# Attention of a two-layer block on one core: the rows of softmax shifts are turned by VectorE in 32x32 squares instead of by TensorE and ScalarE, both parts of the maxima are made by VectorE instead of GpSimd, and the PSUM bank of a score tile rotates by head without a wrap

## The chip, the core and the metric

The kernel runs on 1 core of a Trainium2 chip. The metric is device time in microseconds (us) of one execution. An engine is TensorE (PE; its weight loads are PEld), VectorE (DVE), ScalarE (ACT), GpSimd (POOL) or SyncE (SP, which issues most DMAs).

## The reference, cut to what matters

Two layers on 2048 tokens of width 128: a state-space layer with a routed feed-forward part, then attention with a second routed part. The change touches the attention alone:

```
q, k = rope(x @ Wq + bq), rope(x @ Wk + bk)     # 16 heads of width 8, 2048 tokens
p    = softmax(q @ k.T / sqrt(8))               # per head, 2048 x 2048
out  = concat(p @ v) @ Wo + bo
```

The kernel takes each query's largest score off before the exponential, as a softmax must where scores may be large.

## The kernel before, in words

**Three matmul streams a head.** `q_stack` and `k_stack` hold q and k of one head split in bfloat16 parts; the upper 64 partitions hold one half of the queries, the lower 64 the other, so that two matmuls with 64 rows of weights can run beside each other.
1. *Maxima* (`maxima`, L945): 64 score tiles of 128 queries x 512 keys per head (`SN = 64`), each in one PSUM bank. They serve to find each query's largest score. Head h+1's tiles are made while head h is worked on, 8 tiles in advance: two of them in each entry (below), the *upper* one ahead of the entry's score matmuls and the *lower* one behind them. After the first head they use a ring of three banks (4, 5, 6; `bank_of`), and `free` makes TensorE wait, before it writes a tile, until the tile three places back has been read.
2. *Scores* (`scores`, L956): for each of 16 key tiles (`kt`) and each half of the queries (`hf`), two matmuls give 128 keys x 1024 queries in two banks. One such (kt, hf) is an *entry*; a head has 32. The banks are used in two *slots* that alternate. ScalarE makes the exponentials of an entry in one instruction (L1339).
3. *Values* (`values`, L966): float32 matmuls of the exponentials with v, some entries later.

**Reading the maxima.** In program order of each eight tiles (p = 0 to 7 of a group): ScalarE reads p0 (a rectifier, `above`, L1331); VectorE reduces p1 to p5 and p7 to a column of maxima (L2044), and joins p6 with ScalarE's p0 in one instruction (L2040). VectorE so reads seven tiles of eight. After 32 tiles (`row_maxima`, called after p = 33) and after 64 it reduces the columns of half a head to one maximum for each query (`row_max`, 128 x 8, L2020).

**From maxima to shift rows.** The maxima stand one to a partition and are wanted as rows of `q_stack`, so that the score matmul subtracts them. GpSimd splits `row_max` in a high and a low bfloat16 part (`row_maxima` in its `attention`, L1535 and L1537, into `max_parts`). TensorE then turns 16 columns into 16 rows with a matmul against the identity (`row`, L951), which takes one of the two slots for a moment; ScalarE copies the 16 x 128 result to `shift_rows` (`row`, L1323); SyncE loads it into two places of `q_stack` (`load_rows`, L581; for the second half of head 0 ScalarE issues this load). This stands twice in a head, after `kt` 8 and after `kt` 14 (`ROWS_AFTER`), between two entries on TensorE and on ScalarE; the head then has 34 entries (`ENTRIES`), counted by `s2_ps` and `p_ready`. TensorE waits for the rows (`rows_in`) before entries 0 and 1 of the head that uses them.

**Order around it.** All engines run lists written out by hand, in order. SyncE's list for head h is: store head h-1, load both row halves of head h+1, wait for the last score of head h, load q and k of head h+4. Head 0's tiles are made ahead of the loop with six banks, with ScalarE and VectorE reading in turn; its first row stands after p = 44 (`FIRST_ROW`), its second after three tiles of head 1.

**The ring at a head's end.** The bank of tile p of head hs is

```
4 + (hs % UN + p) % RING        # UN = 4, RING = 3, 64 tiles a head
```

so tile 63 of heads 3, 7 and 11 and tile 0 of the next head have the same bank.

Of the kernel before, what the change touches and what calls it, by code (L numbers as in the profile page):

```python
# [31 lines left out]
TPC = C // 128  # L32
# [86 lines left out]
WIDES = [3, 9]  # L119
PADS = 6  # L120
# [47 lines left out]
ROWS_AFTER = (8, 14)  # L168
FIRST_ROW = SN // 2 + 12
ABOVE = 3  # L170
ROWS = 2 * SHIFT * TPC
ROW_LOADS = 16 * 2

# [5 lines left out]
def bank_of(hs, p):  # L179
    return 4 + (hs % UN + p) % RING if hs else FIRST_BANKS[p % len(FIRST_BANKS)]  # L180
# [32 lines left out]
ENTRIES = 2 * KT + 2  # L213


def entry(kt, hf, rows=True):
    return 2 * kt + hf + (rows and sum(kt > after for after in ROWS_AFTER))


ROW = [entry(after, 1) + 1 for after in ROWS_AFTER]  # L220


# [4 lines left out]
def build(nc, xT_in, cols_in, mats_in, wmod_in, bcsel_in, router_in, digits_in, cos_in, sin_in, spread_in, place_in, moe_in, out):  # L227
    with ExitStack() as ctx:
# [98 lines left out]
        max_parts = sb("max_parts", [128, 2, 2, SHIFT, TPC], BF16)  # L327
# [182 lines left out]
        row_max_ready, max_hi_ready, max_parts_ready = (sem(n) for n in ("row_max_ready", "max_hi_ready", "max_parts_ready"))  # L510
# [94 lines left out]
        def _(sp):  # L605
# [27 lines left out]
            def attention():  # L633
# [36 lines left out]
                load_rows(sp, 0, 0, 0, 3)  # L670
# [20 lines left out]
                for h in range(NH):  # L691
                    if h:
                        store_head(h - 1)
                    if h + 1 < NH:
                        for hf in range(2):
                            load_rows(sp, h + 1, (h + 1) % UN, hf, h * ENTRIES + (ROW[hf] + 5))
                    if h + UN < NH:
                        sp.wait_ge(s2_ps, h * ENTRIES + ENTRIES + 2)
                        load_q(sp, h + UN, h % UN)
                        load_k(sp, h + UN, h % UN)  # L700
# [39 lines left out]
        def _(pe):  # L740
# [171 lines left out]
            def attention():  # L912
# [46 lines left out]
                def values(h, u, kt, rows, part=None):  # L959
# [3 lines left out]
                    pe.wait_ge(p_ready, h * ENTRIES + (entry(kt, 1, rows) + 5))  # L963
# [7 lines left out]
                def late_values(h, u, kt, hf, rows):  # L971

                    at = 2 * kt + hf
                    if at == 0 and h:
                        values(h - 1, (u - 1) % UN, KT - 2, True, 1)
                    elif at == 1 and h:
                        values(h - 1, (u - 1) % UN, KT - 1, True)
                    elif at == 3:
                        values(h, u, 0, rows)
                    elif at > 4:  # L980
                        values(h, u, kt - 2 + hf, rows, 1 - hf)

                def head(h, u, turn, following=NH):
# [7 lines left out]
                    for kt in range(KT):  # L991
                        for hf in range(2):
# [3 lines left out]
                            n = entry(kt, hf, following)  # L996
                            if kt == 0:
                                pe.wait_ge(rows_in[hf], h * ROW_LOADS + ROW_LOADS)
                            pe.wait_ge(p_ready, h * ENTRIES + (n + 3))
# [3 lines left out]
                            late_values(h, u, kt, hf, following)  # L1003
                        if following and kt in ROWS_AFTER:
                            hf = ROWS_AFTER.index(kt)
                            row(h + 1, hf, h * ENTRIES + (2 + ROW[hf]), ROW[hf] % 2)
                for p in range(SN):
                    if p == FIRST_BANKS.index(1):
                        pe.wait_ge(v_all_ready, TILES)
                    if p == FIRST_ROW:  # L1010
                        row(0, 0, 0, 0)
                    maxima(0, 0, p)
                for p in range(RING):
                    maxima(1, 1, p)
                row(0, 1, 1, 1)
                for p in range(RING, 2 * LEAD):
# [3 lines left out]
                values(NH - 1, UN - 1, KT - 2, False, 1)  # L1020
                values(NH - 1, UN - 1, KT - 1, False)

            def attention_out():
                busy(psum[:, 4, :], 26)
                pe.wait_ge(inv_ready, 1)
                pe.wait_ge(p_ready, 2 + 2 + ENTRIES * NH - 2)
# [140 lines left out]
        def _(act):  # L1167
# [139 lines left out]
            def attention():  # L1307
# [25 lines left out]
                def exponentials(h, kt, hf, rows=True):  # L1333
                    n = entry(kt, hf, rows)
                    slot = n % 2
                    act.wait_ge(s2_ps, h * ENTRIES + (n + 3))
# [10 lines left out]
                for p in range(SN):  # L1347
                    if p == FIRST_ROW:
                        row(0, 0, 0, 0)
# [3 lines left out]
                row(0, 1, 1, 1)  # L1353
                load_rows(act, 0, 0, 1, 4)
                for h in range(NH):
                    following = h + 1 < NH
                    for kt in range(KT):
# [3 lines left out]
                        for hf in range(2):  # L1361
                            exponentials(h, kt, hf, following)
                        if kt == 0 and h:
                            keep(h - 1)
                        if following and kt in ROWS_AFTER:
                            hf = ROWS_AFTER.index(kt)
                            row(h + 1, hf, h * ENTRIES + (2 + ROW[hf]), ROW[hf] % 2)
# [75 lines left out]
        def _(pool):  # L1443
# [43 lines left out]
            def attention_inputs():  # L1487
                pool.wait_ge(ln_in_ready, 3 * NC)
                g.memset(no_shift[:], 0.0).then_inc(pool_made, 1)
                g.memset(v_head[:], 0.0).then_inc(pool_made, 1)  # L1490
# [29 lines left out]
            def attention():  # L1520
# [6 lines left out]
                def row_maxima(hs, hf):  # L1527
                    n = hs * 2 + (hf + 1)
                    tiles = slice(8 * hf, 8 * hf + 8)
                    pool.wait_ge(row_max_ready, n)  # L1530
                    if hs:

                        pool.wait_ge(s2_ps, hs * ENTRIES + (2 - ENTRIES))
                    whole, (high, low) = row_max[:, tiles, 0].rearrange("p (d j) -> p d j", j=TPC), (max_parts[:, hf, :, n, :] for n in range(SHIFT))
                    g.tensor_tensor(high, whole, no_shift[:], ALU.add).then_inc(max_hi_ready, 1)  # L1535
                    pool.wait_ge(max_hi_ready, n)
                    g.tensor_tensor(low, whole, high, ALU.subtract).then_inc(max_parts_ready, 1)  # L1537

                def head(h, u, more=True):
                    for hf in range(2):  # L1540
                        row_maxima(h, hf)
# [58 lines left out]
        def _(dve):  # L1600
# [410 lines left out]
            def attention():  # L2011
# [3 lines left out]
                def row_maxima(hs, hf):  # L2015
                    tiles = slice(8 * hf, 8 * hf + 8)
                    dve.wait_ge(s1_read, reads(hs, SN // 2 * (hf + 1)))
                    dve.wait_ge(max_parts_ready, hs * 2 + (hf + 1))
                    tops = tile_max if hs else first_max
                    v.tensor_reduce(row_max[:, tiles, 0], tops[:, tiles, :], AX.X, ALU.max).then_inc(row_max_ready, 1)  # L2020

# [7 lines left out]
                def head(hs):  # L2029
                    for p in range(SN):  # L2030
# [22 lines left out]
                for h in range(NH):  # L2053
                    head(h)
                dve.wait_ge(o_in, 32)
# [101 lines left out]
```

## Time and profile before

| what | us |
|---|---|
| time, median of 3 runs (lowest to highest) | 1195.78 (1195.12 to 1197.62) |
| span of the profiled execution, first to last instruction | 1191.5 |
| attention's steady part, 16 heads, in the profiled execution | about 429 to 1025 |
| busy in the span: TensorE, VectorE, ScalarE, GpSimd | 1039.4, 853.0, 798.2, 291.2 |

No separate time is given for the profiled execution; its span is 4.3 us below the median of the runs. A busy share is a mean over stages with different limits, so the attention has to be read by itself; engines that are busy the same share of a stretch can still be bounded by only one of them.

### The profile page before, as it was taken

What the parts mean: (1) busy time and instruction counts of PE and PEld (TensorE: products, weight loads), DVE (VectorE), ACT (ScalarE), POOL (GpSimd) and SP (SyncE); (2) the same over time, 40 slices, a digit from 0 to 9 for tenths busy, and PEclk for the clock granted to TensorE, in tenths of its full rate; (3) what the DMA queues carried; (4) which work ended last, traced back from release to release, by engine and by line L of the source; (5) the groups of instructions that cost most, each with busy time, mean ns of one, the idle gap of its engine ahead of it and who ended that gap; (6) DMA issues with size and microseconds to landing.
All of it is one profiled execution on the core that took longest, in us unless ns stands there. A gap on an engine that the chain in (4) does not pass through costs nothing.

```text
span 1191.5 us, 22203 instructions
## 1 busy us (share of the span) xinstructions
PE 1039.4 (87%) x8296; PEld 485.1 (41%) x8300; DVE 853.0 (72%) x1585; ACT 798.2 (67%) x1206; POOL 291.2 (24%) x296
## 2 busy tenths in 40 slices
PE   9936767787989689999999999999999999968795
PEld 6512224786964222222222222222222222448694
DVE  2499997347135689999999999999999992362222
ACT  2653333455545469999999999999999999431122
POOL 0069881655334500000000000000000000026652
PEclk7969998889888879999999999999999999988997
DMA  3056530866642310011100111001110100038683
GB/s 104 1 166 195 179 122 36 260 189 201 186 136 88 122 61 25 12 34 34 34 16 20 34 34 34 9 27 34 34 34 2 33 4 4 4 126 266 204 268 124
DMA packets 49110, 104.16 MB, mean 87 GB/s; under 512 B 9440, under 2 KB 11864, under 8 KB 48620
## 3 DMA queue, kind: packets, MB, share of 16 engines
q1 hardware_dynamic: 43386, 91.76, 24.6%
q0 software_dynamic: 4544, 9.32, 2.4%
q10 hardware_dynamic: 1074, 1.67, 0.4%
q8 instruction: 66, 1.08, 0.4%
q14 instruction: 40, 0.33, 0.1%
HBM read 89.35 MB, written 12.94 MB: 86 GB/s over the span
## 4 chain that ended last, share of the span: by engine, by line
PE 61%; issue 12%; DVE 9%; ACT 9%; DMA 4%; POOL 2%; another core or an unknown queue 1%; SPq 1%; ACTq 0%; DVEq 0%; POOLq 0%
PE psum L966 19%; PE psum L945 12%; PE psum L956 8%; PE psum L1085 6%; PE psum L1096 6%; ACT probs L1339 5%; DVE tile_max L2044 2%; DVE ssm_h L1764 1%; PE psum L789 1%; PE psum L1068 1%; PE psum L769 1%; DMA y_in<-y_dram 1%; ACT ln_xn L1331 1%; POOL h0T L1483 1%
## 5 line engine op out<-in xcount | busy, mean ns | idle before, releaser
L1339 ACT ACTIVATE probs<-psum 128x1024 f32<-128x1024 f32 x512 | 504.2, 1041 | 27.6 <-PE psum L956 22.3
L2044 DVE TENSOR_REDUCE tile_max<-psum 128x1 f32<-128x512 f32 x720 | 459.8, 685 | 31.8 <-PE psum L945 25.1
L945 PE MATMUL psum<-k_stack,q_stack 62*128 62x512 bf16 x994 | 313.3, 388 | 14.1 <-DMA q_stack<-q_dram 8.6
L966 PE MATMUL psum<-probs,v_head 128*32 128x256 f32 (+1 forms) x3840 | 321.0, 406 | 0.6 <-ACT probs L1339 0.4
L956 PE MATMUL psum<-q_stack,k_stack 64*128 64x512 bf16 x1024 | 290.0, 384 | 10.6 <-ACT probs L1339 8.7
L945 PEld LDWEIGHTS psum<-k_stack,q_stack 62*128 62x128 bf16 x994 | 77.4, 94 | 242.7 <-issue 109.7
L966 PEld LDWEIGHTS psum<-probs,v_head 128*32 128x32 f32 x3840 | 75.7, 108 | 164.6 <-issue 126.0
L1535 POOL TENSOR_TENSOR max_parts<-row_max,no_shift 128x8 bf16<-128x8 f32 x32 | 6.4, 200 | 557.0 <-DVE row_max L2020 557.0
L1096 PE MATMUL psum<-w2r,hid 128*128 128x128 f32 x624 | 92.5, 296 | 25.4 <-issue 25.2
L1085 PE MATMUL psum<-x_cols,w1r 128*128 128x128 f32 (+1 forms) x624 | 93.5, 299 | 8.8 <-issue 8.0
L1096 PEld LDWEIGHTS psum<-w2r,hid 128*128 128x128 f32 x624 | 84.3, 210 | 28.0 <-issue 27.6
L1085 PEld LDWEIGHTS psum<-x_cols,w1r 128*128 128x128 f32 x624 | 86.0, 213 | 10.7 <-issue 9.8
L1418 ACT ACTIVATE hid<-psum 128x512 f32<-128x512 f32 x39 | 23.0, 597 | 94.3 <-PE psum L1085 49.0
L1483 POOL TENSOR_TENSOR h0T<-dtuT,ssm_b 128x1024 f32<-128x1024 f32 x32 | 76.9, 2414 | 16.4 <-DVE ssm_h L1764 7.3
L1570 POOL DMA_INDIRECT y_dram<-o_rows,put_row x64 | 62.9, 983 | 68.4 <-ACT o_rows L1388 36.4
L1562 POOL DMA_INDIRECT x_got<-xtok_dram,get_row x64 | 63.0, 984 | 52.9 <-issue 34.3
L850 PE MATMUL psum<-ssm_g,mats 128*128 128x512 f32 x128 | 62.7, 614 | 11.5 <-POOL ssm_g L1457 6.4
L2040 DVE CUSTOM_DVE_ANT_0 proj_o<-psum,ln_xn 128x512 f32<-128x512 f32 x100 | 67.8, 684 | 6.5 <-PE psum L945 6.3
L1331 ACT ACTIVATE ln_xn<-psum 128x512 f32<-128x512 f32 x100 | 58.9, 593 | 18.7 <-PE psum L941 11.8
L956 PEld LDWEIGHTS psum<-q_stack,k_stack 64*128 64x128 bf16 x1024 | 55.2, 94 | 36.8 <-ACT probs L1339 31.3
L1900 DVE COPY o_rows<-psum 128x128 f32<-128x128 f32 x39 | 11.3, 290 | 80.7 <-PE psum L1096 44.1
L1246 ACT ACTIVATE psum<-dtT,negA 128x1024 f32<-128x1024 f32 x32 | 35.4, 1109 | 28.6 <-DVE ssm_h L1764 19.0
(287 smaller groups left out, 1107.5 us busy)
## 6 DMA issues: line engine op xcount, KB each, us to landing
w1r<-w SPq DMA_DIRECT2D x78, 256.0 KB
w2r<-w SPq DMA_DIRECT2D x78, 256.0 KB
ssm_b<-bc_dram SPq DMA_DIRECT2D x32, 512.0 KB, 4.0
k_stack<-k_dram SPq DMA_DIRECT2D x60, 120.0 KB
y_in<-y_dram SPq DMA_DIRECT2D x16, 256.0 KB, 5.1
q_stack<-q_dram SPq DMA_DIRECT2D x30, 96.0 KB
bc_p<-bc_dram SPq DMA_DIRECT2D x5, 512.0 KB, 5.7
xtok_dram<-x_tok SPq DMA_DIRECT2D x8, 256.0 KB, 2.4
```

The lines of the kernel that those rows point to most:

```text
L945: mm(bank, queries, k_stack[rows, u, keys:keys + C], start=True, stop=True).then_inc(s1_ps, 1)
L956: return mm(psum[:, 2 * slot + side, :], k_stack[rows, u, kt * 128:(kt + 1) * 128], q_stack[rows, u, hf * C:(hf + 1) * C], start=True, sto ...
L966: i = mm(psum[32 * j:32 * j + VM, 7, lo:hi], v_head[:, u, kt, :], probs[:, kt % 4, j * C + lo:j * C + hi], start=kt == 0, stop=kt == KT - ...
L1085: j = mm(psum[:, n % 3, hc * 128:(hc + 1) * 128], w1r[:, k, hc * 128:(hc + 1) * 128], space, start=True, stop=True)
L1096: j = mm(psum[:, 6 + n % 2, 0:128], hid[:, n % 2, hc, :], w2r[:, k, hc, :], start=hc == 0, stop=hc == HC - 1)
L1331: f(above_next[n % ABOVE], psum[:, bank_of(hs, p), :], ACT.Relu).then_inc(above_ready, 1)
L1339: f(probs[:, kt % 4, hf * HALF:(hf + 1) * HALF], banks(2 * slot, 2), ACT.Exp, scale=SCALE).then_inc(p_ready, 1)
L1483: g.tensor_tensor(ssm_dBu[:, n % 2, :], half(dtuT, hf), ssm_b[:, n % B_RING, :], ALU.mult).then_inc(dBu_ready, 1)
L1562: g.indirect_dma_start(x_got[:, k, :], None, xtok_dram, bass.IndirectOffsetOnAxis(get_row[:, i:i + 1], 0)).then_inc(got[k], 16)
L1570: g.indirect_dma_start(y_dram, bass.IndirectOffsetOnAxis(rows, 0), o_rows[:, k, :], None).then_inc(put[k], 16)
L2040: v.tensor_tensor_reduce(proj_o[:, r % 2, :], bank, above_next[r % ABOVE], 1.0, LOWEST, ALU.add, ALU.max, top).then_inc(s1_read, 1)
L2044: v.tensor_reduce(top, bank, AX.X, ALU.max).then_inc(s1_read, 1)
```

## The change

The matmul, the copy and the entry for a row go. VectorE makes the high and the low part (two `tensor_tensor` of 128 x 8) into a zeroed 128 x 32 tile `max_squares`, and turns this tile with four 32 x 32 transposes, one for each 32 partitions, into 32 partitions of `shift_rows`, of which 16 are used. These instructions stand in VectorE's list of tile reads: for the first half behind p = 34 (high), 35 (low) and 36 (four transposes); for the second half behind p = 0, 1 and 2 of the next head. After head 15's last tile the second half's follow directly. The loads wait for `max_turned`. A head has 32 entries again. The bank uses `hs` instead of `hs % UN`. GpSimd clears `max_squares` once and no longer takes part.

```diff
-ROWS_AFTER = (8, 14)
-FIRST_ROW = SN // 2 + 12
+TURN_AFTER = (SN // 2 + 4, 2)
+SQUARE = 32
+SQUARES = 128 // SQUARE
 def bank_of(hs, p):
-    return 4 + (hs % UN + p) % RING if hs else FIRST_BANKS[p % len(FIRST_BANKS)]
+    return 4 + (hs + p) % RING if hs else FIRST_BANKS[p % len(FIRST_BANKS)]
-ENTRIES = 2 * KT + 2
+ENTRIES = 2 * KT
-        max_parts = sb("max_parts", [128, 2, 2, SHIFT, TPC], BF16)
+        max_squares = sb("max_squares", [128, 2, SQUARE], BF16)
+        max_parts = max_squares[:, :, 0:ROWS].rearrange("p h (d s j) -> p h d s j", d=2, s=SHIFT)
...
-        def load_rows(eng, h, u, hf, done):
-            eng.wait_ge(p_ready, done)
+        def load_rows(eng, h, u, hf):
+            eng.wait_ge(max_turned, SQUARES * (2 * h + hf + 1))
...
-                def row(hs, hf, g, slot):
-                    pe.wait_ge(max_parts_ready, hs * 2 + (hf + 3))
-                    pe.wait_ge(p_ready, g + 1)
-                    mm(psum[0:ROWS, 2 * slot, 0:128], max_parts[:, hf].rearrange("p d s j -> p (d s j)"), ident_b[:],
-                       start=True, stop=True).then_inc(s2_ps, 1)
...
-                def row(hs, hf, g, slot):
-                    act.wait_ge(s2_ps, g + 1)
-                    if hs:
-                        act.wait_ge(rows_in[hf], hs * ROW_LOADS)
-                    f(shift_rows[0:ROWS, hf, :], psum[0:ROWS, 2 * slot, 0:128], ACT.Identity).then_inc(p_ready, 1)
...
-                def row_maxima(hs, hf):
-                    pool.wait_ge(row_max_ready, n)
...
-                    g.tensor_tensor(high, whole, no_shift[:], ALU.add).then_inc(max_hi_ready, 1)
-                    pool.wait_ge(max_hi_ready, n)
-                    g.tensor_tensor(low, whole, high, ALU.subtract).then_inc(max_parts_ready, 1)
...
+                def part_maxima(hs, hf, low):
...
+                    if low:
+                        dve.wait_ge(max_parts_ready, 2 * n + 1)
+                        v.tensor_tensor(rest, whole, high, ALU.subtract).then_inc(max_parts_ready, 1)
+                        return
+                    dve.wait_ge(row_max_ready, n)
+                    if hs:
+                        dve.wait_ge(max_turned, SQUARES * (n - 2))
+                    v.tensor_tensor(high, whole, no_shift[:], ALU.add).then_inc(max_parts_ready, 1)
+                def turn_maxima(hs, hf):
+                    dve.wait_ge(max_parts_ready, hs * 4 + (hf * 2 + 4))
+                    if hs:
+                        dve.wait_ge(rows_in[hf], hs * ROW_LOADS)
+                    for g in range(SQUARES):
+                        at = slice(SQUARE * g, SQUARE * (g + 1))
+                        v.transpose(shift_rows[0:SQUARE, hf, at], max_squares[at, hf, :]).then_inc(max_turned, 1)
...
                         if p == SN // 2 + 1:
                             row_maxima(hs, 0)
+                        for k in range(2):
+                            if p == SN // 2 + 2 + k:
+                                part_maxima(hs, 0, k)
+                            if p == k and hs:
+                                part_maxima(hs - 1, 1, k)
+                        if p == TURN_AFTER[0]:
+                            turn_maxima(hs, 0)
+                        if p == TURN_AFTER[1] and hs:
+                            turn_maxima(hs - 1, 1)
```

## Rows read from the trace of the kernel before

Time and busy columns are in us from the span's start, means in ns. In a timeline an answer's line is: start, length, engine, line, operation, tiles and sizes, count, and in brackets the idle time before it and what ended it.

**Rows 1.** The page's first part: busy time, share of the span, instructions.
```profile
PE 1039.4 (87%) x8296; PEld 485.1 (41%) x8300; DVE 853.0 (72%) x1585; ACT 798.2 (67%) x1206; POOL 291.2 (24%) x296
```

**Rows 2.** Busy time of one head: us, busy PE, PEld, DVE, ACT, POOL, clock, DMA.
```profile
565.30:602.70 37.40, 36.73 (x375) 10.21 (x370) 35.20 (x67) 35.37 (x44) 1.06 (x5) 1.00 0.09 28
```

**Rows 3.** The page's second costliest group: busy, mean of one, idle before it.
```profile
L2044 DVE TENSOR_REDUCE tile_max<-psum 128x1 f32<-128x512 f32 x720 | 459.8, 685 | 31.8 <-PE psum L945 25.1
```

**Rows 4.** TensorE's timeline, two entries without a row: upper tiles, values.
```profile
571.49 0.39 PE L945 MATMUL psum<-k_stack,q_stack 62*128 62x512 bf16 x1
...
572.60 0.39 PE L945 MATMUL psum<-k_stack,q_stack 62*128 62x512 bf16 x1
...
573.16 0.64 PE L966 MATMUL psum<-probs,v_head 128*32 128x256 f32 x8
573.73 0.39 PE L945 MATMUL psum<-k_stack,q_stack 62*128 62x512 bf16 x1
```

**Rows 5.** TensorE's timeline around the second row (L951) of a head.
```profile
577.05 0.39 PE L945 MATMUL psum<-k_stack,q_stack 62*128 62x512 bf16 x1
...
578.19 0.39 PE L945 MATMUL psum<-k_stack,q_stack 62*128 62x512 bf16 x1
...
579.18 0.22 PE L951 MATMUL psum<-ident_b,max_parts 128*16 128x128 bf16 x1
579.33 0.39 PE L945 MATMUL psum<-k_stack,q_stack 62*128 62x512 bf16 x1
579.99 0.39 PE L956 MATMUL psum<-q_stack,k_stack 64*128 64x512 bf16 x2 [0.27 <-ACT probs L1339]
...
581.09 0.39 PE L945 MATMUL psum<-k_stack,q_stack 62*128 62x512 bf16 x1
```

**Rows 6.** ScalarE's timeline at the same row.
```profile
579.79 0.25 ACT L1323 ACTIVATE shift_rows<-psum 16x128 bf16<-16x128 f32 x1
580.42 1.02 ACT L1339 ACTIVATE probs<-psum 128x1024 f32<-128x1024 f32 x1 [0.38 <-PE psum L956]
```

**Rows 7.** VectorE's timeline: a group's only gap, then a head's second row maximum.
```profile
574.15 0.69 DVE L2044 TENSOR_REDUCE tile_max<-psum 128x1 f32<-128x512 f32 x1 [0.17 <-PE psum L945]
...
576.55 0.68 DVE L2040 CUSTOM_DVE_ANT_0 proj_o<-psum,rope_sin 128x512 f32<-128x512 f32 x1
...
577.16 0.69 DVE L2044 TENSOR_REDUCE tile_max<-psum 128x1 f32<-128x512 f32 x1
577.88 0.19 DVE L2020 TENSOR_REDUCE row_max<-tile_max 128x8 f32<-128x32 f32 x1
577.98 0.68 DVE L2044 TENSOR_REDUCE tile_max<-psum 128x1 f32<-128x512 f32 x1
```

**Rows 8.** TensorE's timeline at the end of head 3's tiles (same bank twice).
```profile
538.16 0.64 PE L966 MATMUL psum<-probs,v_head 128*32 128x256 f32 x8
539.67 0.37 PE L945 MATMUL psum<-k_stack,q_stack 62*128 62x512 bf16 x1 [0.87 <-DVE tile_max L2044]
```

**Rows 9.** The chain of waits, first and last of three like pieces.
```profile
535.83 1.43 DVE tile_max L2044 x3
...
837.01 1.43 DVE tile_max L2044 x3
```

**Rows 10.** VectorE's timeline far ahead of the attention: small operations, each waiting for the last.
```profile
241.97 0.16 DVE L1944 TENSOR_TENSOR thr_low<-thr_low,thr_add 128x1 int32<-128x1 int32 x1
242.17 0.16 DVE L1935 TENSOR_TENSOR thr_try<-thr_low,digits 128x1 int32<-128x1 int32 x1
```

**Rows 11.** The chain of waits at the start of the head loop.
```profile
424.87 0.20 DVE row_max L2020
...
426.23 0.75 ACTq L581
```

**Rows 12.** SyncE's timeline: the last load of head 1's k, then head 0's first rows.
```profile
414.09 0.29 SPq L575 DMA_DIRECT2D k_stack<-k_dram  x1
417.18 1.39 SPq L581 DMA_DIRECT2D q_stack<-shift_rows  x2
```

More of the change, by code:

```diff
@@ L210, with entry @@
 JOINED_READ = [reads(hs, p + 1) for hs in range(NH) for p in range(SN) if order_of(hs)[p][3] == JOINED]
-ENTRIES = 2 * KT + 2
-def entry(kt, hf, rows=True):
-    return 2 * kt + hf + (rows and sum(kt > after for after in ROWS_AFTER))
-ROW = [entry(after, 1) + 1 for after in ROWS_AFTER]
+ENTRIES = 2 * KT
+def entry(kt, hf):
+    return 2 * kt + hf
 def half_tiles(hf):
@@ L957, in scores, with values @@
                               q_stack[rows, u, hf * C:(hf + 1) * C], start=True, stop=True)
-                def values(h, u, kt, rows, part=None):
+                def values(h, u, kt, part=None):
                     if kt == 0:
@@ L962, in values @@
                         pe.wait_ge(o_copied, h + 1)
-                    pe.wait_ge(p_ready, h * ENTRIES + (entry(kt, 1, rows) + 5))
+                    pe.wait_ge(p_ready, h * ENTRIES + (entry(kt, 1) + 3))
                     lo, hi = (0, C) if part is None else (part * C // 2, (part + 1) * C // 2)
@@ L1002, in head @@
                             lower()
[L1003 to L1006, printed above, removed]
+                            late_values(h, u, kt, hf)
                 for p in range(SN):
@@ L1009, in attention @@
                         pe.wait_ge(v_all_ready, TILES)
-                    if p == FIRST_ROW:
-                        row(0, 0, 0, 0)
                     maxima(0, 0, p)
[L1013 to L1016, printed above, removed]
+                for p in range(2 * LEAD):
                     maxima(1, 1, p)
@@ L1019, in attention @@
                     head(h, h % UN, h // UN, following=NH - 1 - h)
-                values(NH - 1, UN - 1, KT - 2, False, 1)
-                values(NH - 1, UN - 1, KT - 1, False)
+                values(NH - 1, UN - 1, KT - 2, 1)
+                values(NH - 1, UN - 1, KT - 1)
             def attention_out():
@@ L1331, in above, with exponentials @@
                     f(above_next[n % ABOVE], psum[:, bank_of(hs, p), :], ACT.Relu).then_inc(above_ready, 1)
-                def exponentials(h, kt, hf, rows=True):
-                    n = entry(kt, hf, rows)
+                def exponentials(h, kt, hf):
+                    n = entry(kt, hf)
                     slot = n % 2
-                    act.wait_ge(s2_ps, h * ENTRIES + (n + 3))
+                    act.wait_ge(s2_ps, h * ENTRIES + (n + 1))
                     if hf == 0:
@@ L1352, in attention @@
                 above(1, 0)
[L1353 to L1354 removed]
+                load_rows(act, 0, 0, 1)
                 for h in range(NH):
[L1356 removed]
                     for kt in range(KT):
@@ L1361, in attention @@
                         for hf in range(2):
-                            exponentials(h, kt, hf, following)
+                            exponentials(h, kt, hf)
                         if kt == 0 and h:
                             keep(h - 1)
-                        if following and kt in ROWS_AFTER:
-                            hf = ROWS_AFTER.index(kt)
-                            row(h + 1, hf, h * ENTRIES + (2 + ROW[hf]), ROW[hf] % 2)
                 keep(NH - 1)
@@ L2017, in row_maxima @@
                     dve.wait_ge(s1_read, reads(hs, SN // 2 * (hf + 1)))
-                    dve.wait_ge(max_parts_ready, hs * 2 + (hf + 1))
+                    dve.wait_ge(max_parts_ready, max(hs * 4 + hf * 2, 2))
                     tops = tile_max if hs else first_max
                     v.tensor_reduce(row_max[:, tiles, 0], tops[:, tiles, :], AX.X, ALU.max).then_inc(row_max_ready, 1)
+                def part_maxima(hs, hf, low):
+                    n = hs * 2 + (hf + 1)
+                    tiles = slice(8 * hf, 8 * hf + 8)
+                    whole, (high, rest) = row_max[:, tiles, 0].rearrange("p (d j) -> p d j", j=TPC), (max_parts[:, hf, :, k, :] for k in range(SHIFT))
+                    if low:
[13 more added lines that the diff above has]
+                        v.transpose(shift_rows[0:SQUARE, hf, at], max_squares[at, hf, :]).then_inc(max_turned, 1)
                 bv = mat("bv_rows").rearrange("p (h d) -> p h d", h=NH)
@@ L2054, in attention @@
                     head(h)
+                for k in range(2):
+                    part_maxima(NH - 1, 1, k)
+                turn_maxima(NH - 1, 1)
                 dve.wait_ge(o_in, 32)
```

39 lines of the change are left out of this document (16 added, 23 removed).

## The prediction

> **What bounds the kernel now.** I read the busy totals first: TensorE is busy 87% of the span, VectorE 72%, ScalarE 67% [rows 1]. Then one head by stretch: in 37.4 us TensorE is busy 36.7, ScalarE 35.4 and VectorE 35.2, at a granted clock of 1.00, that is 2.4 GHz [rows 2]. Three engines lie within 2 us of each other, so shares can't tell which is the bound; the timelines must.
>
> TensorE's entries without a row start 1.11 us apart and follow each other without a pause: the values of one take 0.57 us until the next upper tile, the rest is scores and maxima [rows 4]. VectorE reads a tile every 0.60 to 0.61 us, one read takes 0.69 to its end, and in a group of eight tiles it has one gap, 0.17 us [rows 3, 7]. So TensorE sets the pace of an undisturbed group and VectorE is a little faster than it needs to be.
>
> The rows disturb it. With a row, TensorE's scores come 0.66 us behind their upper tile instead of beside it, and two entries take 2.90 us (578.19 to 581.09) instead of 2.22: a row costs 0.68 us [rows 5]. The matmul is only 0.22; the rest is the wait for ScalarE, which has to copy the row (0.25) and then waits itself for the scores (0.38) [rows 5, 6]. Two rows a head make 1.36 us of 37.4.
>
> One more stall stands at a head's end: behind the values the next upper tile comes after 1.51 us instead of 0.57, and 0.87 of it is idle, waiting for VectorE's read [rows 4, 8]. Here tile 63 and the next head's tile 0 have the same bank. The chain of waits shows the stall three times [rows 9].
>
> What is to be seen in that stall is the tightness of the ring: a tile's matmul can start only when the tile three back has been read, and a late read goes into TensorE's time at once, since nothing else can be taken out of its list.
>
> **The change, part by part.**
>
> *Rows off TensorE and ScalarE.* 15 heads follow with two rows each inside the loop: 30 x 0.68 = -20.4 us.
>
> *Bank by head.* Three stalls of about 0.9 go: -2.7 us. Late next would be the tile three back, read long before.
>
> *GpSimd's two operations* run beside everything; nothing is won, since only the row waited for them, and clearing the squares once stands in GpSimd's list ahead of its wait for the tables; without that cover it is one small operation, some 0.2 us.
>
> *VectorE's new work.* First what a small operation costs there. Unhindered, the next read starts 0.10 us behind `row_max`, though that is 0.19 long [rows 7]; I take 0.10 for each part. Where an operation waits for the one ahead, the full length and about 0.04 are paid: small ones of 0.16 follow in 0.20 [rows 10], and `row_max` itself starts 0.72 behind a read instead of 0.61 [rows 7].
>
> The transpose is in no row. Its lower bound is the 0.10 of an unhindered small operation, four of them 0.40. Its upper bound is full length, 0.19 + 0.03 = 0.22 [rows 7]: three such steps and 0.10 for the last, 0.76. Which is nearer? Every pair of VectorE operations that overlaps in this kernel's rows begins at partition 0 on all 128; the four transposes begin at partitions 0, 32, 64 and 96, so the overlap isn't shown for them. I take full length, T = 0.76, and keep 0.40.
>
> The Trainium skill, "VectorE: DVE Perf Modes", section "Two Vector instructions with no wait between them", has a rule on this: an instruction whose input or output starts in another group of 32 partitions than the last one's starts only when all earlier Vector instructions have finished. That speaks against this change; no run here shows it. By the rule T is 0.76, by the row of `row_max` alone 0.40; with the first the sum below is +8, with the second about -4.
>
> *First half of a head.* Take the group whose upper p0 starts at 0. VectorE reads p2 at 1.55 (574.15 less 572.60 [rows 4, 7]); high delays p3 by 0.10, low p4 by another 0.10, the transposes p5 by T. So p6 ends 0.20 + T later than it did. The next group's lower tile p1 needs p6's bank, and before it got it with nothing to spare: p6 is read from 576.55 for 0.68, and the next group's first entry already takes 1.14 instead of 1.11 [rows 4, 5, 7]. The delay goes into TensorE whole: +0.20 + T = 0.96.
>
> *Second half.* High stands directly behind `row_max`, with no read between, and waits for it: p1 moves from 577.98 to about 578.20. Then p1 0.60, low 0.10: p2 at 578.90. Before, p2 could start when its tile was there, 578.19 + 0.39 [rows 5] + about 0.03 = 578.61. That is +0.29, and T on top: +1.05. The gap that would have taken 0.17 was already used by `row_max`.
>
> Each head: 0.96 + 1.05 - 1.36 = +0.65; VectorE's work of 2.0 us exceeds what TensorE is freed of. For 15 heads +9.8 us.
>
> *Loads.* The last transpose of the second half ends at about 578.90 + 0.60 + 0.66 + 0.22 = 580.38; ScalarE's copy ended at 580.04 [rows 6]. SyncE's load so starts 0.34 later, and it is the next thing in that queue either way; TensorE wants the rows 0.37 later too (1.05 less 0.68), so the margin stays. VectorE's added waits, on the loads of a head ago, are over when it comes to them. Behind them its own tile reads are queued, and TensorE waits for those.
>
> *The start.* Head 0's second row now needs high, p1, low, p2 and the transposes behind `row_max`: about 0.22 + 0.10 + 0.60 + 0.10 + 0.60 + 0.88 = 2.5 us, where the load was issued 1.36 us behind it (424.87 to 426.23 [rows 11]): +1.1. Head 0's first half puts up to 0.96 into VectorE's reads. Against that SyncE, which stood idle from 414.38 to 417.18 for head 0's first row [rows 12], gets it earlier, and heads 2 and 3's loads move up by at most 2.8. Bounds -2.8 to +2.1; I take +1.
>
> **Sum:** +9.8 - 2.7 + 1 = +8 us. The profiled execution has a span of 1191.5 and no time of its own; 4.3 us lie between it and the median of the runs, and I take these as unchanged. So, 1195.8 + 8 = **1204 us**.
>
> **The rivals.**
>
> *A, cheap transposes.* They overlap like `row_max` and the read behind it. T = 0.40 gives 0.60 + 0.69 = 1.29 a head against 1.36: -1 in 15 heads, and with the banks, and nothing for the start, about -4: **1192**. This is the rival on the other side. Its place is the four transposes behind p = 36 and behind p = 2, its price 2T a head, and it decides from 15 x (0.49 + 2T - 1.36) - 1.7 = 0, that is T = 0.49. For it: every overlap in the rows. Against: those all stay on the same partitions.
>
> *B, the lag is absorbed.* VectorE has eight gaps of 0.17 a head, 1.36 us [rows 7]. If its lag is worked off in them without holding TensorE, only 2.0 - 1.4 = 0.65 of its new work shows: a head falls by 0.7, 15 heads by 10.7, and with -1.7 the time is **1183**. For it: the totals of the engines, VectorE's head comes to 37.2 us at most by busy time [rows 2]. Against: rows 8, where one late read idles TensorE for 0.87 with the gaps as they are.
>
> *C, the joined read waits too.* If an operation that changes partitions is paid at full length, the read of p6 behind the transposes, which takes ScalarE's tile from partition 0 on, may start 0.1 late as well (the 0.11 of `row_max` [rows 7]): 30 times, +3, **1207**. It is part of the likeliest case's own spread.
>
> **How the numbers follow.** Full length with or without C has 0.60; its own range is 1199 to 1211, from 0.2 a head on the delays and the bounds of the start. A has 0.27 (1189 to 1196), B 0.09; 0.04 is for what I don't see, split. The range that leaves 2 in 10 out goes from A's lower part to the top of the likeliest case: 1190 to 1211. A measurement of this kernel can tell about 0.2%, 2.4 us, from no change. Faster: B and 0.6 of A, 0.25. Within 0.2%: 0.35 of A and the lowest end of the likeliest case, 0.12. Slower: 0.63.
>
> **What the profile of after would show.** TensorE's L951, ScalarE's L1323 and GpSimd's two groups are gone, and no entry's scores start behind their upper tile for want of a slot. Heads no longer differ by 0.9 after heads 3, 7 and 11. VectorE's four transposes in a row start about 0.22 apart (right) or 0.10 (rival A). Behind each set, TensorE's maxima wait for VectorE's reads, about 1 us per half head, and a head takes 38.0 us. If a head takes 37.3 with transposes 0.10 apart, A holds; if transposes are slow and a head still takes under 37, the step that puts VectorE's delay whole into TensorE is wrong. I am wrong altogether if the transposes cost several times their length, or if the rows reach `q_stack` too late and TensorE waits for the load.

## The result and the profile after

The changed kernel is slower: 1201.26 us median (1198.07 to 1211.46, 13 runs) against 1191.30 (1185.09 to 1197.62, 13 runs) of the kernel before on the same chip, a ratio of 1.0090 with a 95% interval of 1.0068 to 1.0112. That is +8 to +13 us, where +8 was forecast.

The two profiled executions lie further apart than the medians, 1209.6 against 1191.5 of span, and part of that is not the change's: the profiled execution of after is the slowest of its 13 runs (1211.46), and GpSimd's first `q_negative`, which closes the work ahead of the attention, ends at 406.26 against 401.43. All comparisons below start there. From that point to the reciprocal of the softmax sums at the attention's end, the kernel before takes 629.45 and the one after 642.25: **+12.8 us**. With the 4.8 ahead of it and 0.5 behind it, that is the 18.1 between the spans. One execution of each is not a mean: a run below whose edit leaves the start alone shows a start 1.7 longer than before's, so +12.8 and the +10 of the medians don't disagree.

The page of after, its first part and two groups (busy, mean ns of one, idle before it and what ended most of it):

```profile
PE 1046.0 (86%) x8264; PEld 484.2 (40%) x8268; DVE 876.8 (72%) x1777; ACT 802.6 (66%) x1174; POOL 279.9 (23%) x233
...
L2024 DVE TENSOR_REDUCE tile_max<-psum 128x1 f32<-128x512 f32 x720 | 458.0, 681 | 25.9 <-PE psum L946 24.7
...
L946 PEld LDWEIGHTS psum<-k_stack,q_stack 62*128 62x128 bf16 x994 | 79.9, 93 | 291.5 <-DVE tile_max L2024 182.5
```

The last group in the page of before:

```profile
L945 PEld LDWEIGHTS psum<-k_stack,q_stack 62*128 62x128 bf16 x994 | 77.4, 94 | 242.7 <-issue 109.7
```

The tile reads cost what they cost before (681 ns against 685 [rows 3]), but 192 instructions have joined them on VectorE (1777 against 1585 [rows 1]): 16 heads x 2 halves x 6. The weight loads name the victim: TensorE's for the maxima now sat idle mostly for VectorE's reads (182.5 of 291.5), where before the largest part (109.7 of 242.7) had no wait that the profile shows ("issue").

One head, from its first exponential to that of the next (busy by engine as in [rows 2]):

```profile
593.60:631.90 38.30, 37.20 (x372) 10.21 (x374) 36.57 (x79) 35.73 (x42) 0.32 (x1) 1.00 0.09 27
```

38.30 against 37.42, at the same clock. VectorE is busy 1.37 longer than before (36.57 against 35.20), TensorE 0.47 (37.20 against 36.73), and TensorE now stands idle for 1.10 of the head where it was 0.67. The waits of two heads, before (565 to 640) and after (594 to 668), each with its sum in us, its count and the longest:

```profile
PEld psum L945 <- DVE tile_max L2044: 12.3, 27, 0.8
```

```profile
PEld psum L946 <- DVE tile_max L2024: 23.0, 50, 0.9
```

The weight loads wait twice as often for VectorE. Where that comes from is seen in VectorE's timeline after a first half's maximum:

```profile
608.88 0.16 DVE L1992 TENSOR_TENSOR max_squares<-row_max,no_shift 128x8 bf16<-128x8 f32 x1
608.96 0.68 DVE L2024 TENSOR_REDUCE tile_max<-psum 128x1 f32<-128x512 f32 x1
609.56 0.16 DVE L1987 TENSOR_TENSOR max_squares<-row_max,max_squares 128x8 bf16<-128x8 f32 x1
609.63 0.68 DVE L2024 TENSOR_REDUCE tile_max<-psum 128x1 f32<-128x512 f32 x1
610.23 0.88 DVE L2000 STREAM_TRANSPOSE shift_rows<-max_squares 32x32 bf16<-32x32 bf16 x4
611.05 0.64 DVE L2024 TENSOR_REDUCE tile_max<-psum 128x1 f32<-128x512 f32 x1
611.72 0.69 DVE L2020 CUSTOM_DVE_ANT_0 proj_o<-psum,ln_xn 128x512 f32<-128x512 f32 x1
```

The parts cost 0.08 and 0.07 each: the read behind one starts so soon although the part is 0.16 long. The four transposes hold the engine from 610.23 to the next read at 611.05, **0.82**. And the joined read (L2020) starts 0.67 behind its predecessor, 0.03 after that one's end, where reads of before follow in 0.60 to 0.61 [rows 3, 7]. In heads 1 to 13 all 26 joined reads behind transposes start 0.03 after their predecessor's end, and all 78 others 0.08 before it. TensorE pays at the upper tiles:

```profile
610.07 0.39 PE L946 MATMUL psum<-k_stack,q_stack 62*128 62x512 bf16 x1
...
611.75 0.39 PE L946 MATMUL psum<-k_stack,q_stack 62*128 62x512 bf16 x1 [0.41 <-ACT probs L1318]
...
613.37 0.39 PE L946 MATMUL psum<-k_stack,q_stack 62*128 62x512 bf16 x1
```

Two entries take 1.68 and 1.62 instead of 1.11 [rows 4]: +1.08. (The bracket names ScalarE, but the upper tile at 611.75 is p = 40 and needs the bank of p = 37, whose read ended at 611.05 + 0.64 = 611.69. The lower tile behind it, at 612.48, needs that of p = 38, the joined read, which ended at 611.72 + 0.69 = 612.41.) In the second half three entries from 627.86 on take 1.67, 1.49 and 1.33: +1.16. Together 2.24, less the 1.36 of the two rows: +0.88 a head, and heads 1 to 13 all take 38.29 to 38.30. The 38.32 that heads 2, 6 and 10 took before (at their ends the tiles of heads 3, 7 and 11 give way to the next head's) is gone with the repeated bank.

At the start, the chain of waits shows the transposes one by one, then the load of head 0's second row (start, us, what):

```profile
430.20 0.20 DVE row_max L1979
430.40 0.02 issue
430.42 0.17 DVE max_squares L1992
430.59 0.60 DVE tile_max L2024
431.19 0.07 DVE max_squares L1987
431.26 0.60 DVE tile_max L2024
431.86 0.11 DVE shift_rows L2000
431.97 0.03 issue
432.00 0.20 DVE shift_rows L2000
432.20 0.03 issue
432.23 0.18 DVE shift_rows L2000
432.41 0.06 issue
432.46 0.21 DVE shift_rows L2000
432.67 0.02 issue
432.70 0.75 ACTq L582
433.44 0.04 issue
433.48 6.14 DMA q_stack<-shift_rows
```

Each transpose runs to its end before the next starts: they start 0.23 apart (432.00, 432.23, 432.46). The load is issued 2.50 behind `row_max`, against 1.36 before [rows 11].

Where the +12.8 came from, added up along ScalarE's first exponentials and TensorE's wait for that load: 2.92 up to head 0's second entry, 1.04 from there to head 1, 13 x 0.87 = 11.3 in heads 1 to 13, -2.7 by the banks, and 0.24 in heads 14 and 15. Head 14 by itself doesn't change (36.03 against 36.04).

### The profile page after: what moved, and what is told of

Its sections match the earlier page's. It is cut to its first block, busy times and chain, and to the rows that moved or that the text cites. A ratio compares the mean times of both kernels' runs of the same rounds, so it can differ in the third digit from the quotient of the medians.

```text
span 1209.6 us, 22204 instructions
## 1 busy us (share of the span) xinstructions
PE 1046.0 (86%) x8264; PEld 484.2 (40%) x8268; DVE 876.8 (72%) x1777; ACT 802.6 (66%) x1174; POOL 279.9 (23%) x233
## 3 DMA queue, kind: packets, MB, share of 16 engines
q10 hardware_dynamic: 1074, 1.67, 0.4%
q8 instruction: 66, 1.08, 0.4%
## 4 chain that ended last, share of the span: by engine, by line
PE 59%; DVE 13%; issue 13%; ACT 6%; DMA 4%; POOL 2%; SPq 1%; another core or an unknown queue 0%; ACTq 0%; DVEq 0%; POOLq 0%
PE psum L960 18%; PE psum L946 12%; PE psum L950 7%; PE psum L1071 6%; PE psum L1082 6%; ACT probs L1318 4%; DVE tile_max L2024 2%; DVE proj_o L2020 2%; DVE ssm_h L1723 2%; PE psum L790 1%; PE psum L1054 1%; DVE shift_rows L2000 1%; DMA y_in<-y_dram 1%; PE psum L770 1%; POOL h0T L1455 1%
## 5 line engine op out<-in xcount | busy, mean ns | idle before, releaser
L946 PE MATMUL psum<-k_stack,q_stack 62*128 62x512 bf16 x994 | 320.6, 390 | 26.6 <-ACT probs L1318 12.2
L950 PE MATMUL psum<-q_stack,k_stack 64*128 64x512 bf16 x1024 | 296.8, 385 | 3.8 <-DMA q_stack<-shift_rows 3.4
L946 PEld LDWEIGHTS psum<-k_stack,q_stack 62*128 62x128 bf16 x994 | 79.9, 93 | 291.5 <-DVE tile_max L2024 182.5
L1498 POOL COPY v_head<-v_all 128x144 f32<-128x144 f32 x16 | 5.0, 318 | 476.6 <-PE psum L960 476.6
L1310 ACT ACTIVATE ln_xn<-psum 128x512 f32<-128x512 f32 x100 | 59.0, 594 | 25.3 <-PE psum L946 11.3
L1859 DVE COPY o_rows<-psum 128x128 f32<-128x128 f32 x39 | 11.3, 289 | 81.5 <-PE psum L1082 39.8
L2020 DVE CUSTOM_DVE_ANT_0 proj_o<-psum,ln_xn 128x512 f32<-128x512 f32 x100 | 67.8, 683 | 0.8 <-ACT ln_xn L1310 0.2
L1377 ACT ACTIVATE hid<-psum,block_b 128x128 f32<-128x128 f32 x128 | 36.8, 383 | 26.6 <-PE psum L1071 19.9
```

The costliest lines, as they stand in the source:

```text
L946: mm(bank, queries, k_stack[rows, u, keys:keys + C], start=True, stop=True).then_inc(s1_ps, 1)
L950: return mm(psum[:, 2 * slot + side, :], k_stack[rows, u, kt * 128:(kt + 1) * 128], q_stack[rows, u, hf * C:(hf + 1) * C], start=True, sto ...
L2020: v.tensor_tensor_reduce(proj_o[:, r % 2, :], bank, above_next[r % ABOVE], 1.0, LOWEST, ALU.add, ALU.max, top).then_inc(s1_read, 1)
```

## The experiments

The theory after the result: the four transposes are paid at full length because each reads other partitions than the one before, and whatever VectorE loses there TensorE loses too. Rivals: the parts are what costs (not the transposes); the transposes are that slow anyway; the ring's lead is too short; the start carries the loss (of this the sum above leaves at most 2.92 of 12.8). Each run's times were compared with the kernel before on the same chip; heads are measured between first exponentials.

**The banks alone**, in the kernel before.

```diff
-    return 4 + (hs % UN + p) % RING if hs else FIRST_BANKS[p % len(FIRST_BANKS)]
+    return 4 + (hs + p) % RING if hs else FIRST_BANKS[p % len(FIRST_BANKS)]
```

> The kernel before with the new bank rule alone. Theory: the three stalls at the ends of heads 3, 7 and 11 (0.90 us each, a head of 38.32 against 37.42) go and nothing else moves: all heads 37.42 us, -2.7 us, 0.23% faster than before. Rival: with the wrap gone the lag of VectorE's reads shows elsewhere in those heads and less than 1 us is won.

Measured: 1184.25 against 1186.64, ratio 0.9987 (0.9969 to 1.0005). ScalarE's timeline at the starts of heads 2, 3 and 4 (head 2 is the first that took 38.32 before):

```profile
499.93 1.03 ACT L1339 ACTIVATE probs<-psum 128x1024 f32<-128x1024 f32 x1
...
537.36 1.03 ACT L1339 ACTIVATE probs<-psum 128x1024 f32<-128x1024 f32 x1
...
574.78 1.03 ACT L1339 ACTIVATE probs<-psum 128x1024 f32<-128x1024 f32 x1
```

37.43 and 37.42, and so are all heads from 1 to 13: the three stalls go, -2.7 us in the trace, and no head is longer in their place. The time can't tell -2.7 from nothing, since its interval holds both 0.9977 and 1. In this execution the way to head 1 was 1.7 longer than before's (70.25 against 68.54), which no part of the edit touches, so stretches at the start differ by that much between executions.

**Four transposes that all read partitions 0 to 31.**

```diff
-SCALE = float(HD) ** -0.5
+SCALE = 0.05
...
-    v.transpose(shift_rows[0:SQUARE, hf, at], max_squares[at, hf, :]).then_inc(max_turned, 1)
+    v.transpose(shift_rows[0:SQUARE, hf, at], max_squares[0:SQUARE, hf, :]).then_inc(max_turned, 1)
```

> The changed kernel, but all four transposes read partitions 0 to 31 (so three quarters of the shifts are other queries' maxima, and the exponential's scale is made 0.05 to keep its results finite). Theory: a transpose starts late because it begins at other partitions than the one ahead of it; here the four start 0.10 us apart and the joined read behind them starts 0.60 instead of 0.67 to 0.70 behind its predecessor; a half head gains 3 x 0.12 + 0.1, a head falls from 38.29 to about 37.35 us. Rival: transposes never overlap; they start 0.22 apart as in the changed kernel and a head stays at 38.1 to 38.3.

The shifts of three quarters of the queries are other queries' here, so only the times count. It ran once, 1189.35 against 1186.64, from which nothing follows; in the profiled execution the attention, measured as above, takes 623.54 against before's 629.45. VectorE's timeline in the same place as above:

```profile
563.11 0.68 DVE L2024 TENSOR_REDUCE tile_max<-psum 128x1 f32<-128x512 f32 x1
563.71 0.47 DVE L2000 STREAM_TRANSPOSE shift_rows<-max_squares 32x32 bf16<-32x32 bf16 x4
564.11 0.64 DVE L2024 TENSOR_REDUCE tile_max<-psum 128x1 f32<-128x512 f32 x1
564.68 0.67 DVE L2020 CUSTOM_DVE_ANT_0 proj_o<-psum,rope_sin 128x512 f32<-128x512 f32 x1
```

The same four instructions now take 0.40 (563.71 to 564.11) instead of 0.82, each 0.09 to 0.12 behind the last, and the joined read starts 0.57 behind its predecessor instead of 0.67. Heads take 37.21 instead of 38.29: 1.08 less, of which 2 x 0.42 are the transposes and 2 x 0.10 the joined reads. The only other edit is the scale inside ScalarE's exponentials, so the change of partitions is the price, of both. This is also rival A's case made on the chip: at T = 0.40 a head is 0.21 shorter than the 37.42 of before.

The Trainium skill, "VectorE: DVE Perf Modes", section "Two Vector instructions with no wait between them", says that an instruction is held until all earlier ones have finished when an input starts in another group of 32 partitions than the last input read from the same memory. The traces agree in each part: the second to fourth transposes are held, the first isn't; the read behind them (its input in PSUM) isn't; the joined read, the next to read SBUF, is, and it reads from partition 0 where the last transpose read from 96. The prediction told the rule as a comparison with the last instruction, whatever that one read; by those words the read of PSUM behind the transposes would be held too, and it starts 0.06 before the last transpose ends.

**The parts back on GpSimd**, transposes kept.

```diff
+    g.tensor_tensor(high, whole, no_shift[:], ALU.add).then_inc(max_parts_ready, 1)
+    pool.wait_ge(max_parts_ready, 2 * n + 1)
+    g.tensor_tensor(low, whole, high, ALU.subtract).then_inc(max_parts_ready, 1)
...
-    for k in range(2):
-        if p == SN // 2 + 2 + k:
-            part_maxima(hs, 0, k)
-        if p == k and hs:
-            part_maxima(hs - 1, 1, k)
```

> The changed kernel with the high and the low part made by GpSimd again; VectorE keeps the transposes. Theory: what VectorE no longer does comes off TensorE's stalls whole: 0.20 us in the first half, 0.22 + 0.10 in the second; a head falls from 38.29 to about 37.8, the kernel by 7 to 8 us against the changed one, to about no difference from before. Rival: VectorE then waits for GpSimd ahead of the transposes and a head stays at 38.3 or grows.

Measured: 1193.49 against 1186.64, ratio 1.0072 (1.0045 to 1.0099); heads 37.89. The parts so cost 0.40 of a head on VectorE, and without them the change is still slower than before. The rival that the parts are the whole loss falls. The head is as expected, the time is not: about no difference from before was expected, and heads of 37.89 against 37.42 alone make 13 x 0.47 - 2.7 = +3.4. The start makes the rest. It was longer than in any run but one (head 1 at 72.89): GpSimd's first high part, behind its own 5.46 us addition to `xT`, came at 409.30 where `row_max` was at 404.97, and VectorE's transposes waited for it (68.54 to head 1 in before).

**The first half's work spread to VectorE's gaps**: high behind p = 41, low behind 49, transposes behind 57, where a group's first read has 0.17 to spare [rows 7].

```diff
-TURN_AFTER = (SN // 2 + 4, 2)
+TURN_AFTER = (SN // 2 + 25, 2)
...
-    if p == SN // 2 + 2 + k:
+    if p == SN // 2 + 9 + 8 * k:
         part_maxima(hs, 0, k)
```

> The changed kernel with the first half's work at other places: high behind p = 41, low behind p = 49, the four transposes behind p = 57, each where VectorE has its 0.17 us gap in a group. Theory: only the lag that the gap doesn't take reaches TensorE: high and low cost nothing, the transposes 0.17 less; the first half's stall falls from 1.08 to about 0.7, a head from 38.29 to about 37.9, the kernel by 5 to 6 us against the changed one. Rival: what counts is VectorE's work in sum, wherever it stands; a head stays at 38.3.

Measured: 1189.75 against 1186.64, ratio 1.0038 (1.0022 to 1.0053); heads 37.87, that is 0.42 less than after. VectorE's timeline around the part and the transposes:

```profile
600.00 1.28 DVE L2024 TENSOR_REDUCE tile_max<-psum 128x1 f32<-128x512 f32 x2
601.20 0.16 DVE L1987 TENSOR_TENSOR max_squares<-row_max,max_squares 128x8 bf16<-128x8 f32 x1
601.45 2.48 DVE L2024 TENSOR_REDUCE tile_max<-psum 128x1 f32<-128x512 f32 x4
...
605.66 0.88 DVE L2000 STREAM_TRANSPOSE shift_rows<-max_squares 32x32 bf16<-32x32 bf16 x4
606.48 2.43 DVE L2024 TENSOR_REDUCE tile_max<-psum 128x1 f32<-128x512 f32 x4
608.94 0.69 DVE L2020 CUSTOM_DVE_ANT_0 proj_o<-psum,ln_xn 128x512 f32<-128x512 f32 x1
```

Behind the part the next read starts at 601.45, 0.17 after the end of the reads ahead (600.00 + 1.28), which is the gap of a group without it [rows 7]: there the part costs nothing. The transposes take 0.82 here too, and a gap of 0.17 takes back little of that. The joined read is late again: it starts 0.03 behind the end of the four reads between (606.48 + 2.43), where in the undisturbed group it starts 0.08 ahead of that end.

**GpSimd's addition to `xT` later.** In the trace of after, one instruction is out of line: the first high part of head 0. GpSimd's and VectorE's timelines there:

```profile
415.96 5.45 POOL L1509 TENSOR_SCALAR xT<-xT,gated_bo 128x2048 f32<-128x2048 f32 x1
...
417.75 1.96 DVE L1992 TENSOR_TENSOR max_squares<-row_max,no_shift 128x8 bf16<-128x8 f32 x1
419.62 0.68 DVE L2020 CUSTOM_DVE_ANT_0 proj_o<-psum,ln_xn 128x512 f32<-128x512 f32 x1
420.23 0.08 DVE L2020 DVE_READ_ACCUMULATOR2_ANT first_max<- 128x1 f32 x1
420.23 0.15 DVE L1987 TENSOR_TENSOR max_squares<-row_max,max_squares 128x8 bf16<-128x8 f32 x1
```

1.96 instead of 0.16, while GpSimd adds. The edit moves the addition into the loop over heads, at h = 2:

```diff
-    g.tensor_scalar(xT[:], xT[:], gated_bo[:], None, ALU.add).then_inc(x_biased, 1)
...
+    if h == 2:
+        g.tensor_scalar(xT[:], xT[:], gated_bo[:], None, ALU.add).then_inc(x_biased, 1)
```

> The changed kernel with GpSimd's 5.45 us addition to xT moved behind its copies of v for heads 2 to 4. Theory: head 0's first high part took 1.96 us instead of 0.16 because GpSimd's long operation ran beside it and VectorE's two-input operation had to wait for it; with that moved it takes 0.16 to 0.2, and the way from the end of GpSimd's q_negative to the first exponential is about 1.8 us shorter (29.4 to about 27.6 us, give or take the landing of loads); heads stay at 38.29. The moved addition may now hold one such operation of VectorE in the loop for up to 2 us. Rival: the first operation of its kind is slow whatever runs beside it; it stays at 1.96.

```profile
410.91 0.16 DVE L1993 TENSOR_TENSOR max_squares<-row_max,no_shift 128x8 bf16<-128x8 f32 x1
```

The part takes 0.16, the first exponential comes after 27.56 instead of 29.36, head 1 after 69.91 instead of 72.50, and heads stay at 38.29. So the two did collide, for 1.8. The time doesn't show it: 1201.69 against 1189.62, ratio 1.0101 (1.0061 to 1.0141), an interval that holds after's whole.

**One transpose of all 128 partitions** from head 1 on, 128 x 32 into 128 x 32, with eight small loads a half in place of two; the parts and the transposes at places with a gap; and, since the rows come later, a lead of eight entries.

```diff
-LEAD = 4
-TURN_AFTER = (SN // 2 + 4, 2)
+LEAD = 8
+TURN_AFTER = (SN // 2 + 25, 5)
...
+    for g in range(SQUARES):
+        first = SQUARE * g + side * SHIFT * TPC
+        part = to.rearrange("s (j g c) -> s j g c", g=SQUARES, c=SQUARE)[:, :, g, :]
+        eng.dma_start(part, shift_rows[first:first + SHIFT * TPC, hf, 0:SQUARE]).then_inc(rows_in[hf], 16)
...
+    v.transpose(shift_rows[:, hf, 0:SQUARE], max_squares[:, hf, :]).then_inc(max_turned, 1)
...
-    if p == SN // 2 + 2 + k:
+    if p == SN // 2 + 9 + 8 * k:
...
-    if p == k and hs:
+    if p == k + 1 and hs:
```

> The changed kernel with, from head 1 on, one transpose of 128 x 32 in place of four of 32 x 32 (the rows then stand in four places of 32 partitions and are loaded by eight DMAs for each half instead of two), the tiles made 16 instead of 8 in advance so that the loads have time, the first half's work in the gaps (high behind 41, low 49, transpose 57), the second's behind p = 1, 2 and 5. Theory: a transpose that stays on its partitions costs VectorE 0.1, and work in a gap costs nothing; a head keeps 37.42 - 1.36 and some 0.3 of the second half: 36.3 to 36.6 us, -13 to -16 us in 15 heads, -2.7 for the banks, +2 to +4 for eight more tiles ahead of the loop: 1.0 to 1.4% faster than before. Rival: the 16 DMA issues a head (0.65 us each on SyncE) land too late for entry 1 or collide with the stores, and heads stay above 37.4.

Measured: **1178.07 against 1189.62, ratio 0.9914 (0.9883 to 0.9946)**: faster than both kernels. VectorE's timeline at a first-half and a second-half transpose, then the head that begins at 570.26:

```profile
564.28 0.20 DVE L2015 STREAM_TRANSPOSE shift_rows<-max_squares 128x32 bf16<-128x32 bf16 x1
564.40 0.65 DVE L2039 CUSTOM_DVE_ANT_0 proj_o<-psum,ln_xn 128x512 f32<-128x512 f32 x1
...
593.61 0.20 DVE L2015 STREAM_TRANSPOSE shift_rows<-max_squares 128x32 bf16<-128x32 bf16 x1
```

```profile
570.26:606.82 36.56, 36.43 (x376) 10.28 (x368) 35.12 (x73) 35.42 (x42) 0.32 (x1) 1.00 0.10 28
```

One transpose of 128 partitions is as long as one of 32 (0.20), in the first half the next instruction, the joined read, starts 0.12 behind it and is on time. A head takes 36.56: 1.73 less than after, 0.86 less than before, and 1.0 above the 35.5 of 32 undisturbed entries. VectorE is busy 35.12 instead of 36.57. The 240 small loads stall TensorE little (0.5 us in two heads). How much of the 1.73 is the one transpose and how much the places isn't measured apart; the spread of the first half with four transposes gave 0.42.

The time fell by less than the 1.0 to 1.4% expected. In the profiled execution the attention takes 613.38 against 629.45, 16.1 less, but that execution is the fastest of the six (1170.60; the others 1176.39 to 1181.83); what the others lost has no trace.

**The lead alone**, in the kernel after (`LEAD = 8` and ScalarE's first reads to match), as the control.

```diff
-LEAD = 4
+LEAD = 8
...
-    above(1, 0)
+    for p in range(0, 2 * LEAD, GROUP):
+        above(1, p)
```

> The changed kernel with the tiles made 16 instead of 8 in advance and nothing else. Theory: where tiles stand in a head's entries doesn't matter to the ring, a head stays at 38.3; the first exponential comes later by about eight tiles, at most 5 us, part of which is given back at head 0's entry 1, that waits less for its rows, and at the end. Rival: the loads of the second half's rows were close to late; with more time for them heads shrink by some tenths.

Its one time is 1201.35: heads 38.29 to 38.30 as in after, and the attention 642.32 against 642.25. A longer lead brings the first exponential 4.64 later (34.00 against 29.36 behind `q_negative`), shortens head 0 by 3.38 (39.76 against 43.14) and head 14 by 1.04 (34.99 against 36.03), and changes nothing between. So the lead by itself gains nothing, and what the run with one transpose gained is put down to the transposes and the places; whether it would have held with a lead of four was not run.

## Why the prediction was right

- **Rows off TensorE and ScalarE, -0.68 each: consistent.** The row's entry was not measured alone, but with the delays read off TensorE's timeline it closes the head: 2.24 - 1.36 = 0.88 against 0.87 measured.
- **Banks, -2.7: right.** Shown in both kernels that have the edit.
- **Transposes at full length: right**, and the choice that decided the sign. T was 0.82 where 0.76 was taken, since the steps are 0.22 to 0.23 and the last one costs more than an unhindered small operation. At equal partitions T was 0.40, the other end to the hundredth, and a head then came to 37.21 where the prediction's working gives 37.35.
- **The parts: nearly right.** 0.10 was taken, 0.07 to 0.08 shown; taking them off saves 0.40 of a head against 0.49 in the sum.
- **VectorE's delay goes whole into TensorE: right.** +1.08 and +1.16 against 0.96 and 1.05. What is missing, 0.1 in each half, is the joined read's hold (0.07 by after's timeline, 0.10 by the run with equal partitions); T's 0.06 more and the parts' 0.05 less nearly cancel, which is luck. Rival C named that with its price, and it stood outside the sum at +3 us; the runs make it part of the sum, and with it the forecast would have been 1207 by its own working. So the sum's mis-sized term is that one: +0.65 a head forecast, +0.87 measured. The sum also counted fifteen heads; head 14 showed none of it.
- **Rivals A and B: refuted.** The transposes don't overlap, and a head rose by 0.87 where B had it fall by 0.7. Work has to be put at a gap to use it: the spread of the first half gave back 0.42 of a head, while in the order of after the first half's whole 1.04 (0.08 + 0.07 + 0.82 and 0.07 for the joined read) shows in TensorE as 1.08.
- **The start: +1 forecast, +2.92 measured** up to head 0's second entry, where it waits for the load. The 2.50 from `row_max` to the load was forecast as 2.5 and accounts for 1.14. Its transfer took 6.14 instead of 4.86, another 1.28, and `row_max` itself came 0.50 later (after 23.94 against 23.44). Neither of these two is shown to be the change's. With the banks alone, where nothing of the start was edited, `row_max` came after 23.92, and the same transfer, here in the chains of before and of that run, took longer too:

```profile
427.01 4.86 DMA q_stack<-shift_rows
```

```profile
418.32 5.69 DMA q_stack<-shift_rows
```

Over the eight executions in whose chain it stands it took 4.86 to 6.28. Against the run with the banks alone the start is +1.61, inside the prediction's bounds of -2.8 to +2.1; against before's execution it is outside. What the change did bring, and the prediction missed altogether, is the collision with GpSimd, 1.80: `row_max` comes after 23.94 in after and after 22.14 with the addition moved. Without it, VectorE's start would have been 1.3 ahead of before's 23.44, within the bounds given.

Against medians: the prediction's base was 1195.78, three runs that lie above most later runs of the same kernel (1191.30 of 13). The forecast of +8 stands against +10 by the medians and +12.8 in the profiled attention. That 1204 lies only 2.7 above the measured 1201.26 is partly luck: a base 4.5 too high and a change 2 too small offset each other.

## What to carry to other kernels

When a short operation is added to a list that other engines wait on, price it at start-to-start distance, and look which partitions it and its neighbours read from: four transposes from four starting partitions cost 0.82 here, from one starting partition 0.40, and one transpose of all 128 partitions 0.12, with small DMAs doing the rearranging instead. Then place it behind an instruction that is followed by a gap, and follow the delay through the ring of buffers to the engine that pays. An operation moved to another engine also meets the neighbours there, here a long GpSimd instruction at the start.

## What the runs showed of the hardware that was not expected

A hold reaches past instructions that read another memory: the joined read was late (0.03 after its predecessor's end) with one read of PSUM between it and the transposes, and still in the spread run, where four lie between.

The first high part started 1.79 into GpSimd's 5.45 us addition and ended 3.75 after that addition's start (417.75 + 1.96 less 415.96). In the run with equal partitions the part started 2.24 in (413.22 to 415.46) and lasted 1.50, which ends it at 3.74; in the run with the lead alone it started 1.83 in (405.22 to 407.05) and lasted 1.91, again 3.74; in the spread run it started 3.53 in (405.65 to 409.18) and took 0.21, 3.74 once more. In the run with one transpose it started 3.96 in (402.16 to 406.12) and took 0.16, and after's low part, 4.27 in, took 0.15, both with GpSimd's instruction still running. `row_max`, which has one input, ran 1.02 in and took its usual 0.19 (416.98 in after). So in these runs a VectorE operation with two inputs in SBUF that starts early ends 3.74 into the 5.45, which less its own 0.16 puts its release at about 3.6 (an estimate), not at the end. The profile's spans on GpSimd are rough, but the engine did stay busy: in before its next instruction, whose input was there at 412.28, started 5.42 after the addition did (410.63 to 416.05). That the two meet at a shared way to SBUF is not shown by a run. The Trainium skill, "SBUF — State Buffer", section "Who interferes with whom", says that a VectorE instruction with two SBUF inputs contends with a GpSimd instruction that reads SBUF; the collision agrees. Its section "SBUF: two separate sides" says that whichever of the two starts first keeps the shared pair of ports for the whole instruction; the release at about 3.6 of 5.45 does not agree with that.
